# An LSTM step with two late values in PSUM, one group of matmuls moved forward, and edge indices copied one unit early

## The reference, cut to what matters

```python
# graph layer: for each edge, the features and the score of its source node
h_src = h[src]
scores = h_src @ a_s + h_tgt @ a_t
ex = exp(scores - mx[tgt]); se = segment_sum(ex, tgt)
agg = segment_sum(h_src * (ex / se[tgt])[:, None], tgt)

# mixer: 4 layers of linear attention and an FFN on the same 6250 rows
x1 = x + gnn(xn, edges) + mix(xn)

# LSTM: 6250 steps, one after the other, state of 256
def step(carry, xp):
    h, c = carry
    gates = xp + h @ W_hh.T                  # 256 x 1024, float32
    i, f, g, o = split(gates, 4)
    c = sigmoid(f) * c + sigmoid(i) * tanh(g)
    h = sigmoid(o) * tanh(c)
    return (h, c), h
```

## Time and profile before

| | us |
|---|---|
| median of 3 runs | 14610.48 |
| profiled execution, its own time | 14609.96 |
| its span in the trace | 14608.1 |
| outside the span | 1.9 |
| TensorE busy | 12774.0 |
| VectorE busy | 6897.3 |
| ScalarE busy | 6966.2 |
| GpSimd busy | 2888.3 |

### The profile page before, as it was taken

One profiled execution on the slowest core, in us unless ns is written; L12 is line 12 of the kernel. 1 busy time (PEld: TensorE's weight loads), 2 busy tenths in 40 slices (PEclk: granted clock), 3 DMA queues, 4 the chain that ended last, 5 costly groups with the idle time before them and its releaser, 6 DMA issues. The chain is left out here.

```text
span 14608.1 us, 1970394 instructions
## 1 busy us (share of the span) xinstructions
PE 12774.0 (87%) x904808; PEld 11330.5 (78%) x904808; DVE 6897.3 (47%) x48363; ACT 6966.2 (48%) x42405; POOL 2888.3 (20%) x4596
## 2 busy tenths in 40 slices
PE   3697878877699999999999999999999999999998
PEld 2585766756588888888888888888888888888886
DVE  5868677675533333333333333333333333333335
ACT  2474655555144444444444444444444444444443
POOL 5675767667000000000000000000000000000000
PEclk7898999988899999999999999999999999999998
DMA  4454545545200000000000000000000000000000
GB/s 91 126 149 122 144 127 140 134 131 139 93 3 2 2 2 2 2 2 2 2 2 2 2 2 2 2 2 2 2 2 2 2 2 2 2 2 2 2 2 19
DMA packets 692139, 542.15 MB, mean 37 GB/s; under 512 B 545207, under 2 KB 595929, under 8 KB 679740
## 3 DMA queue, kind: packets, MB, share of 16 engines
q1 hardware_dynamic: 469456, 315.98, 8.6%
q0 software_dynamic: 221600, 223.50, 6.5%
q10 hardware_dynamic: 934, 0.99, 0.0%
HBM read 286.02 MB, written 252.14 MB: 37 GB/s over the span
## 5 line engine op out<-in xcount | busy, mean ns | idle before, releaser
L1490 PE MATMUL p_g<-ring,wh 128*32 128x16 f32 x800000 | 8209.7, 186 | 693.7 <-DVE ring L1589 601.3
L1490 PEld LDWEIGHTS p_g<-ring,wh 128*32 128x32 f32 x800000 | 7598.1, 110 | 1469.1 <-DVE ring L1589 1152.7
L1531 ACT ACTIVATE cell<-p_g 128x3 f32<-128x3 f32 x12500 | 2173.5, 174 | 5562.7 <-PE p_g L1490 5562.7
L1583 DVE CUSTOM_DVE_ANT_1 cj<-cell 128x4 f32<-128x4 f32 x12500 | 2038.9, 163 | 5667.3 <-ACT cell L1531 5667.3
L1624 POOL COPY hist<-ring 128x6 f32 x2501 | 471.5, 189 | 10382.2 <-POOLq L1623 10382.2
L1534 ACT ACTIVATE tc<-cell 128x1 f32<-128x1 f32 x12500 | 2482.0, 199 | 0.0
L1589 DVE SCALAR_TENSOR_TENSOR ring<-og,tc 128x1 f32<-128x1 f32 x12500 | 1991.9, 159 | 778.4 <-ACT tc L1534 1.9
L423 POOL DMA_INDIRECT eb<-node_tab,eidx x1650 | 2141.1, 1298 | 687.0 <-issue 419.1
L1536 ACT ACTIVATE og<-p_g 128x1 f32<-128x1 f32 x12500 | 2046.4, 170 | 2.0 <-PE p_g L1490 1.8
L1464 PE MATMUL p_g<-xq,idn 128*32 128x24 f32 (+3 forms) x80032 | 1615.2, 189 | 61.6 <-PEq L1477 15.4
L1464 PEld LDWEIGHTS p_g<-xq,idn 128*32 128x32 f32 x80032 | 1254.8, 110 | 231.4 <-issue 15.6
(11 more groups left out here) (220 smaller groups left out, 7049.2 us busy)
## 6 DMA issues: line engine op xcount, KB each, us to landing
edge_tab<-eb SPq DMA_DIRECT2D x98, 1019.8 KB
edge_tab<-eb SPq DMA_DIRECT2D x96, 566.6 KB
edge_tab<-eb SPq DMA_DIRECT2D x96, 339.9 KB
eb<-node_tab,eidx POOLq DMA_INDIRECT x1650
xp_tab<-xo SPq DMA_DIRECT2D x50, 500.0 KB, 2.6
xq<-xp_tab SPq DMA_DIRECT2D x1251, 8.0 KB, 1.7
xq<-xp_tab SPq DMA_DIRECT2D x1250, 12.0 KB, 1.7
edge_tab<-eb SPq DMA_DIRECT2D x98, 118.4 KB
```

The source lines that it names most:

```text
L1490: m = pe.matmul(to[32 * q:32 * q + 32], wh[:, k, D * q + 32 * c:D * q + 32 * c + 32], ring[:, (s - 1) % TS, k:k + 1].broadcast_to([128, w] ...
L1531: act.activation(cell[:, s, k, 0:6:2], gate_at(h, u, k)[:, :, 0], ACT.Tanh).then_inc(l_s[k], 1)
L1583: dve.tensor_tensor_reduce(cj[:, k, :].rearrange("p (a b) -> p a b", a=2), cell[:, s, k, 0:4].rearrange("p (a b) -> p a b", a=2), cell[:, ...
```

## The change

Three edits.

1. **Edge indices.** `eidx` has eight buffers instead of four. The copy of the next unit's indices is issued right behind the first gather of the present unit, always UC = 9 indices, with a semaphore of its own (`e_idx`); the gather of the next unit waits for it together with `e_free`. `srci` is 9 columns longer, filled with 0, so that the copy behind the last unit reads something. GpSimd's loops have eight units in a body instead of four.
2. **LSTM, TensorE.** `gate(6, 0)` stands ahead of `gate(3..5, 1)`, so ahead of the signal `l_g[1]`.
3. **LSTM, ScalarE and VectorE.** `out_gate(0)` writes to a spare column (504 + u) of the PSUM bank of c 6 instead of `og` in SBUF; `tanh_c(1)` writes to that column in the bank of c 7 instead of `tc` in SBUF. `new_h(0)` and `new_h(1)` read them there. `out_gate(1)` and `tanh_c(0)` go to SBUF as before.

```diff
-                eidx = [sb(ctx, f"eidx{s}", [R, UC], I32) for s in range(NSLOT)]
+                eidx = [sb(ctx, f"eidx{u}", [R, UC], I32) for u in range(2 * NSLOT)]
...
+                def edge_index(pool, u, c0):
+
+                    pool.tensor_copy(eidx[u][:], srci[:, ds(c0, UC)]).then_inc(e_idx, 1)
+
-                def edge_gather(pool, place):
+                def edge_gather(pool, u, place):
 
                     s, c0, n, _ = place
                     pool.wait_ge(e_free[s], 32)
                     pool.sem_inc(e_free[s], -32)
-                    pool.tensor_copy(eidx[s][:, 0:n], srci[:, ds(c0, n)]).then_inc(s_pool, 1)
-                    pool.wait_ge(s_pool, 1)
-                    pool.sem_inc(s_pool, -1)
+                    pool.wait_ge(e_idx, 1)
+                    pool.sem_inc(e_idx, -1)
                     for j in range(n):
                         pool.indirect_dma_start(eb[s][:, j, 0:HW], None, node_tab,
-                                                bass.IndirectOffsetOnAxis(ap=eidx[s][:, j:j + 1], axis=0)).then_inc(e_got[s], 16)
+                                                bass.IndirectOffsetOnAxis(ap=eidx[u][:, j:j + 1], axis=0)).then_inc(e_got[s], 16)
+                        if j == 0:
+                            edge_index(pool, (u + 1) % (2 * NSLOT), c0 + n)
...
-                            for c in (4, 5):
+                            for c in (4, 5, 6):
                                 gate(c, 0)
                             for c in (3, 4, 5):
                                 m = gate(c, 1)
                             m.then_inc(l_g[1], 1)
+                            gate(6, 1).then_inc(l_g[2], 1)
                             for k in range(KC):
-                                gate(6 + k, 0)
-                                gate(6 + k, 1).then_inc(l_g[2 + k], 1)
+                                m = gate(7, k)
+                            m.then_inc(l_g[3], 1)
...
                             def tanh_c(k):
-                                return act.activation(tc[:, (s % 2), k:k + 1], cell[:, (s + 1) % TS, k, 5:6], ACT.Tanh)
+                                to = late_at(h, u, 1) if k else tc[:, s % 2:s % 2 + 1]
+                                return act.activation(to, cell[:, (s + 1) % TS, k, 5:6], ACT.Tanh)
+
                             def out_gate(k):
-                                return act.activation(og[:, (s % 2), k:k + 1], gate_at(h, u, 2 + k)[:, :, 0], ACT.Tanh)
+                                to = og[:, s % 2:s % 2 + 1] if k else late_at(h, u, 0)
+                                return act.activation(to, gate_at(h, u, 2 + k)[:, :, 0], ACT.Tanh)
...
                             def new_h(k):
-                                dve.scalar_tensor_tensor(ring[:, s, k:k + 1], og[:, (s % 2), k:k + 1], 1.0, tc[:, (s % 2), k:k + 1],
+                                gate, th = (og[:, s % 2:s % 2 + 1], late_at(h, u, 1)) if k else (late_at(h, u, 0), tc[:, s % 2:s % 2 + 1])
+                                dve.scalar_tensor_tensor(ring[:, s, k:k + 1], gate, 1.0, th,
```

More of the change, by code:

```diff
@@ L51 @@
 U0 = (EC - DEPTH * NSTEP * UL) // 2
-assert 0 < U0 <= UC and 2 * U0 + DEPTH * NSTEP * UL == EC and NSTEP % NSLOT == 0
+assert 0 < U0 <= UC and 2 * U0 + DEPTH * NSTEP * UL == EC and NSTEP % (2 * NSLOT) == 0
 FC = FF // 128
@@ L397, in gps_kernel @@
             with ExitStack() as ctx:
-                srci = sb(ctx, "srci", [R, EC], I32)
+                srci = sb(ctx, "srci", [R, EC + UC], I32)
                 dstf = sb(ctx, "dstf", [R, EC])
@@ L406, in gps_kernel @@
                 ecar = sb(ctx, "ecar", [R, D])
-                e_init = sem("e_init")
+                e_init, e_idx = sem("e_init"), sem("e_idx")
                 e_got = [sem(f"e_got{s}") for s in range(NSLOT)]
@@ L644, in _ @@
                 def _(sp):
-                    sp.dma_start(srci[:], src_pj).then_inc(s_load, 16)
+                    sp.dma_start(srci[:, 0:EC], src_pj).then_inc(s_load, 16)
                     sp.dma_start(pen[:].bitcast(I32), dst_pj).then_inc(s_load, 16)
@@ L703, in _, with pair_units @@
                         pool.nop().then_inc(e_free[s], 32)
-                    for place in AHEAD:
-                        edge_gather(pool, place)
+                    pool.memset(srci[:, EC:], 0).then_inc(s_pool, 1)
+                    pool.wait_ge(s_pool, 1)
+                    pool.sem_inc(s_pool, -1)
+                    edge_index(pool, 2 * NSLOT - len(AHEAD), 0)
+                    for a, place in enumerate(AHEAD):
+                        edge_gather(pool, 2 * NSLOT - len(AHEAD) + a, place)
+                    def pair_units(layer, which):
+                        with pool.Fori(0, NSTEP // (2 * NSLOT)) as i:
+                            for u in range(2 * NSLOT):
+                                edge_gather(pool, u, unit_place(layer, which, (u % NSLOT, i * 2 + u // NSLOT, i * (2 * NSLOT) + u)))
                     with pool.Fori(0, DEPTH) as layer:
-                        units(pool, layer, 0, lambda place: edge_gather(pool, place))
-                        units(pool, layer, 1, lambda place: edge_gather(pool, place))
-                        units(pool, layer, 2, lambda place: edge_gather(pool, place))
+                        for which in range(len(UNITS)):
+                            pair_units(layer, which)
+                    pool.wait_ge(e_idx, 1)
+                    pool.sem_inc(e_idx, -1)
                     for s in range(NSLOT):
@@ L1394, in gps_kernel @@
                 cell = sb(sub, "cell", [128, TS, KC, 6])
-                og, tc = sb(sub, "og", [128, 2, KC]), sb(sub, "tc", [128, 2, KC])
+                og, tc = sb(sub, "og", [128, 2]), sb(sub, "tc", [128, 2])
                 cj = sb(sub, "cj", [128, KC, 4])
@@ L1423, in gate_at, with late_at @@
                     return p_g[h][n][:, u * (c1 - c0) * W:(u + 1) * (c1 - c0) * W].rearrange("p (c w) -> p c w", w=W)
+                def late_at(h, u, k):
+                    return p_g[h][2 + k][:, 504 + u:505 + u]
                 @block.sync
@@ L1524, in _ @@
                     act.wait_ge(l_z, 1)
-                    act.activation(tc[:, 0, :], tc[:, 1, :], ACT.Tanh)
+                    act.activation(tc[:, 0:1], tc[:, 1:2], ACT.Tanh)
                     with act.Fori(0, IT):
```

## The result

The changed kernel took 14835.09 us (median of 4 runs, 14830.5 to 14844.34) against 14612.44 us before: a ratio of 1.0151, 95% interval 1.0138 to 1.0164, 223 us more. (The median before is now of 4 runs; the first three gave 14610.48.) The forecast was 14806 us, +196 over the profiled execution, with an LSTM term of +250 and an edge term of -54.

What follows compares the result with a forecast made beforehand. The LSTM, 72% of the span, was taken as bounded by loop B, in the edges GpSimd's issue in 9-edge passes; 14609.96 + 250 - 54 = 14806 us, 8-in-10 range 14540 to 15050.

Steps and rivals of the forecast that it cites:

- LSTM term of +250: LSTM steps: 70 - 30 + 0 = 40 ns more a step on loop B, over 6250 steps +250 us.
- edge term of -54: Mixer stage, units of 9 edges: GpSimd saves 0.61 us a unit at about 22 units x 4, 54 us.
- loop B: LSTM step's chain: half-state 1, 64 passes, gates(1), new_c(1), tanh_c(1), new_h(1), half-state 1; claimed to have no idle wait.
- loop A: LSTM chain: gates(1), tanh_c(0), out_gate(0), new_h(0), next step, 32 passes ending about 0.01 us before half-state 1 arrives.
- TensorE's order, +70 ns: LSTM, ahead of l_g[1]: eight more passes at 8.8 ns each add 70 ns a step; bounds 0 and 75.
- `tanh_c(1)` to PSUM, -30 ns: LSTM, ScalarE: the write moved from SBUF to PSUM saves 30 ns, counted once in loop B.
- The range's far end, 110: Upper bound in ns on what one ScalarE write moved to PSUM could save; 199 less 0.09 us.
- `out_gate(0)` to PSUM: LSTM, ScalarE: the write moved to PSUM saves 30 ns, counted once in loop A.
- Loop A grows as much, but half-state 1 still arrives last: LSTM: loop A grows like loop B, by 40 ns a step, but adds nothing to the time.
- Loop C: LSTM chain through the 128th pass, l_g[3], out_gate(1), tanh_c(1); does not grow, so gets 0.07 us of slack.
- VectorE on PSUM, 0: LSTM, new_h reading one operand from PSUM: no change in length; bounds -4 and +90 ns.
- another engine does not take over: Mixer stage: VectorE's 289.2 us of waiting for gathers exceeds GpSimd's 54 us saving, so the saving holds.

Runs made afterwards that it cites:

- a second dose: The changed kernel with c 7 by half-state 0 also moved ahead of the signal for the second gates, eight passes more: 15251.64 us.
- PSUM alone: Kernel before with only the third edit, out_gate(0) and tanh_c(1) written to PSUM; TensorE's order and edges as before: 14476.73 us, ratio 0.9903.
- order alone, no copy: Kernel before with only the second edit, and GpSimd's copy of ring to hist in the LSTM left out: 15037.12 us, ratio 1.0288.

## Why the prediction was right, point by point

The time is close, and the price of the passes was worked out soundly. But the closeness of the LSTM's term, 40 ns forecast and 43 measured, is in part luck. The forecast came from loop B, 70 - 30. The step that closes is loop A's: it started 17 ns lower, took 67 for the passes and lost 5 by the shorter `out_gate(0)`, 45 in the sum. That 17 and 5 come near the 30 is chance.

- **TensorE's order, +70 ns: right.** Measured 73 alone, 66 on top of the other edits, 67 to 68 for a second dose. The pace of 8.8 ns was a little high; eight passes cost 66 to 68.
- **`tanh_c(1)` to PSUM, -30 ns: right for the instruction** (203 to 174 ns), not for the step. With the old order the step gained 17 ns of it (1.675 to 1.658), then loop A closed. With the new one it gained 28 to 30, of which 6 are GpSimd's copy. The range's far end, 110, was never near.
- **`out_gate(0)` to PSUM: the sum did not need it, but the step was wrong.** I let it gain the same 30 ns on loop A. It gains 0 to 5. The saving of a side in PSUM does not add up: 199 ns from SBUF to SBUF, 174 from SBUF to PSUM, 163 to 171 from PSUM to SBUF, 163 with both in PSUM.
- **"Loop A grows as much, but half-state 1 still arrives last": wrong.** That is the step that failed. Half-state 1 is early now, and loop A closes at 1.718 us. Loop B alone would have closed at about 1.710: 55 ns from `new_h(1)` to the 33rd pass, 882 to `gates(1)` (as measured where TensorE waits), 618 to `new_h(1)` and 155 for it. So the mistake cost 3 ns against the forecast 1.715, and 8 against loop B's own length.
- **Loop C was not needed, and never closed a step here.** With the new order `out_gate(1)` begins 66 ns sooner behind `gates(1)` and `tanh_c(1)` begins where it did, 0.41 us behind it: `new_c(1)` had held it already.
- **VectorE on PSUM, 0: right.** 158 and 155 ns against 159. The difference between the Trainium skill's figures of about 60 and 125 ns (Perfetto Trace Analysis, Optimizing Scalar/DVE Operations) does not show in this instruction's length. For ScalarE its direction holds and its doubled difference of 84 ns does not: 199 to 163 is 36.
- **Edges, -54: right** (-56 alone, about -46 in the changed kernel), with two offsetting errors. The copy lies mostly in the gap (0.09 more, not 0.20), so GpSimd saves 0.72 us a unit and not 0.61; and "another engine does not take over" was too simple. VectorE's waits for gathers fell to 169.3, not 235, and most of what they lost came back ahead of the mixer's product.
- The sum, +196 for +223: 19 of the 27 missing are the LSTM's (269 against 250), 8 the edges'.

## What to carry to other kernels

In a closed loop of a few engines, write down every cycle and its slack before pricing an edit: here two lay 17 ns apart and a third took over soon after, so work put ahead of the shared signal cost its full pace, 414 us, while work taken from the same place gave back 11 ns of 66. An edit that bundles a gain and a loss should be run in parts: two of the three edits here give 14421 us, and the third alone turned them into 14835. When a wait shrinks more than the time does, look for the wait that grew. And when a forecast hits, check that the loop it was added up on is the one that closes.

## What the runs showed of the hardware that I had not expected

- An engine's small instruction has no fixed length. `out_gate(0)` with the same operands lasted 168 ns in the kernel before and 163 with TensorE's order alone; `out_gate(1)` lasted 202 ns in the kernel with eight passes more, where it began right behind its twin, against 171:

```profile
9004.11 0.16 ACT L1558 ACTIVATE p_g<-p_g 128x1 f32<-128x1 f32 x1
9004.17 0.20 ACT L1558 ACTIVATE og<-p_g 128x1 f32<-128x1 f32 x1
```

- A copy on GpSimd that began mostly 23 to 26 ns ahead of `new_h(1)`, which writes the buffer that the copy reads, lengthened it from 160 to between 172 and 176 ns; one that began 40 to 43 ns behind it did not (159), nor did one in the changed kernel that began up to 18 ns behind it (155), where `new_h(1)` reads one operand from PSUM.
- A TensorE wait that is not met at once cost 8 ns more than the time waited. With the old order `gates(1)` begins 815 ns behind the 33rd pass where TensorE waits for half-state 1 (before, by 9 ns) and 807 where it does not (PSUM alone). With the new order it is 882 (order alone, no copy; a wait of 16 ns) and 874 (changed kernel).
- ScalarE began its next instruction 93 ns behind `tanh_c(0)`, which reads SBUF, and in the kernel with eight passes more 51 ns behind `out_gate(0)`, which reads and writes PSUM, although the two last 195 and 163 ns there.
